# A hybrid layer on one core: first row of the batch densely through the first mixture, order and filler matmuls changed, last half row densely through the second mixture

## The reference

```
x = x + scan(norm(x))          # state space model, 16 states per feature
x = x + mixture(norm(x))       # 8 experts, top 1, capacity 512
x = x + conv(norm(x))          # two gates and one long convolution
x = x + mixture(norm(x))       # the same weights again
```

```
probs = softmax(x @ Wr + br)
gate, idx = max(probs), argmax(probs)
pos = position of the token among those of its expert, counted from 1
kept where pos < C
h = relu(gate * x @ W1[idx] + b1[idx])
out = gate * (h @ W2[idx] + b2[idx])       # 0 for tokens that aren't kept
```

## Time and profile before

| | us |
|---|---|
| median of three runs | 488.82 |
| fastest and slowest | 488.31, 494.63 |
| the profiled execution | 495.49 |
| its span, first to last instruction | 493.7 |
| busy: PE, DVE, ACT, POOL | 292.3, 343.4, 212.3, 309.2 |

### The profile page before, as it was taken

One profiled execution on the slowest core, in us unless ns is written; L12 is line 12 of the kernel. 1 busy time (PEld: TensorE's weight loads), 2 busy tenths in 40 slices (PEclk: granted clock), 3 DMA queues, 4 the chain that ended last, 5 costly groups with the idle time before them and its releaser, 6 DMA issues.

```text
span 493.7 us, 4946 instructions
## 1 busy us (share of the span) xinstructions
PE 292.3 (59%) x1327; PEld 152.8 (31%) x1327; DVE 343.4 (70%) x794; ACT 212.3 (43%) x346; POOL 309.2 (63%) x218
## 2 busy tenths in 40 slices
PE   4978753588877887970010782439778584036730
PEld 3323310312412412530000551216355583024410
DVE  4798699999999999977260763453787974236520
ACT  2787755246556646511010491334785121015610
POOL 2142189699999999957575002767745647527674
PEclk9999975587787777685555798566799896559965
DMA  7014240840100100106412342110201122132200
GB/s 212 18 69 129 60 127 0 285 195 0 43 0 0 44 0 1 44 1 174 110 44 77 110 152 74 54 43 27 68 13 33 56 66 93 38 110 80 78 23 11
DMA packets 29159, 34.12 MB, mean 69 GB/s; under 512 B 5488, under 2 KB 20862, under 8 KB 29132
## 3 DMA queue, kind: packets, MB, share of 16 engines
q1 hardware_dynamic: 24236, 25.39, 16.7%
q0 software_dynamic: 4096, 7.71, 4.9%
q10 hardware_dynamic: 800, 0.71, 0.5%
HBM read 14.43 MB, written 20.19 MB: 70 GB/s over the span
## 4 chain that ended last, share of the span: by engine, by line
DVE 26%; issue 26%; PE 20%; POOL 8%; ACT 6%; another core or an unknown queue 5%; DMA 3%; DVEq 3%; SPq 2%; ACTq 1%; POOLq 0%
DVE states L825 13%; POOL x L1157 3%; POOL states L810 2%; PE ps L1521 2%; PE ps L1592 2%; ACT scaled L1257 2%; PE ps L1611 2%; PE ps L1062 2%; DVE stats L882 1%; PE ps L691 1%; POOL slots L1036 1%; PE ps L1195 1%; SPq L1409 1%; PE ps L1211 1%
## 5 line engine op out<-in xcount | busy, mean ns | idle before, releaser
L810 POOL TENSOR_TENSOR states<-states,c_rows 128x1024 f32<-128x1024 f32 x60 | 144.5, 2440 | 18.2 <-DVE states L825 17.8
L825 DVE TENSOR_TENSOR_SCAN states<-ps,inp 128x1024 f32<-128x1024 f32 x64 | 140.5, 2261 | 0.4 <-ACT ps L786 0.4
L786 ACT ACTIVATE ps<-ps,bias_p,scale_p 128x1024 f32<-128x1024 f32 x64 | 75.0, 1177 | 64.5 <-PE ps L676 64.2
L1036 POOL DMA_INDIRECT slots<-x,put x64 | 63.9, 999 | 47.1 <-DVE put L1030 28.8
L676 PE MATMUL ps<-stack,sel 96*128 96x512 bf16 x128 | 49.6, 482 | 35.3 <-DVE states L825 35.1
L1157 POOL DMA_INDIRECT x<-answers,put x32 | 30.9, 965 | 45.5 <-DMA answers<-reply 36.5
L1348 POOL DMA_INDIRECT out<-reply,home x32 | 31.6, 988 | 24.9 <-DVE reply L1327 17.0
L691 PE MATMUL ps<-states,red 128*32 128x512 f32 x256 | 41.6, 764 | 2.5 <-POOL states L810 2.5
L1327 DVE SCALAR_TENSOR_TENSOR reply<-ps,rows,kept 128x128 f32<-128x128 f32 x64 | 18.6, 344 | 29.7 <-remote 18.0
L676 PEld LDWEIGHTS ps<-stack,sel 96*128 96x128 bf16 x128 | 8.8, 104 | 75.7 <-DVE states L825 64.7
L882 DVE BATCH_NORM_STATS2 stats<-x 128x6 f32<-128x128 f32 x96 | 19.8, 277 | 14.1 <-DMA x<-answers,put 13.9
(11 more groups left out here) (174 smaller groups left out, 604.5 us busy)
## 6 DMA issues: line engine op xcount, KB each, us to landing
slots<-zero SPq DMA_DIRECT2D x8, 528.0 KB
rows<-slots SPq DMA_DIRECT2D x16, 264.0 KB
steps<-part SPq DMA_DIRECT2D x4, 768.0 KB, 3.3
stack<-steps SPq DMA_DIRECT2D x12, 256.0 KB, 4.2
answers<-x SPq DMA_DIRECT2D x4, 512.0 KB
answers<-reply SPq DMA_DIRECT2D x8, 256.0 KB, 2.6
out<-x SPq DMA_DIRECT2D x4, 512.0 KB
x<-in_x SPq DMA_DIRECT2D x3, 512.0 KB, 5.6
```

The source lines that it names most:

```text
L786: act.activation(bank(ps, slot(b, u), 2), bank(ps, slot(b, u), 2), ACT.Exp, scale=m["scale_p"][:, group(u):group(u) + 1], bias=m["bias_p"] ...
L810: eng.tensor_tensor(h[:, u * SEQ:(u + 1) * SEQ], h[:, u * SEQ:(u + 1) * SEQ], c_rows[:, b * SEQ:(b + 1) * SEQ], ALU.mult).then_inc(done, 1)
L825: dve.tensor_tensor_scan(h[:, u * SEQ:(u + 1) * SEQ], bank(ps, slot(b, u), 2), inp[:, b * SEQ:(b + 1) * SEQ], 0.0, ALU.mult, ALU.add).then ...
L1036: pool.indirect_dma_start(out=m["slots"][n // BATCH], out_offset=bass.IndirectOffsetOnAxis(m["put"][:, b, i:i + 1], 0), in_=m["x"][:, b * ...
```

## The change

- First mixture, row 0 of the batch: it isn't scattered. All 1024 tokens go through all 8 experts as a dense product (class `Dense`): ScalarE scales the rows, TensorE turns them, and in 16 steps (2 halves of 512 tokens, 8 experts) multiplies by w1, adds -2^100 where the token isn't the expert's (a bf16 matmul with `pick`), ScalarE takes the relu, TensorE multiplies by w2 and adds up over experts in PSUM. b2 comes in by the one-hot rows in `turn_back`, and VectorE adds gate times sum to x (`finish`). Rows 1 to 3 are scattered and gathered as before.
- Second mixture: the same for the last 4 tiles (second half of row 3, 8 steps), laid between the experts; they are stored by one more DMA (`store_last`). Row 3 has 4 scatters left.
- "Natural order": each row is counted from the one-hots of all former rows (`count`); `own` and `prior` are gone.
- The first scan unit is moved ahead into `project` on TensorE, ScalarE and VectorE (`begin`).
- `keep_clock`: bf16 matmuls of ones, 128x128 by 512 columns, whose product nothing reads, at several places of TensorE's queue, 68 in all.
- The weights are loaded by SP before x of the first layer is stored, while the scan runs.
- Statistics no longer make `spread` and `neg_mean`: the moments are kept per use, eps comes in as ScalarE's bias.
- Convolution: v times filt_bias is added by TensorE (`bias_diag`, two fp32 matmuls of 512 columns per row) and the first z operation goes. The first row's products move from GpSimd to VectorE. The order of rows on TensorE, ScalarE and VectorE is changed.

The diff, cut to its core:

```diff
+def keep_clock(pe, m, ps, at, n):
+
+    ones = m["ones"][:, :].rearrange("p (o e) -> p o e", o=1).broadcast_to([P, HT, P])
+    for _ in range(n):
+        pe.matmul(bank(ps, at), m["ones"][:, :], ones, start=True, stop=True)
...
     def count(self, pe, n):
...
+        need(pe, self.placed, n)
+        for row in range(b):
+            for i in range(BT):
+                pe.matmul(counts, m["ones"][:, :], m["onehot"][:, row, i:i + 1, :].broadcast_to([P, BT, EXPERTS]), start=row + i == 0, stop=False)
         need(pe, self.hot, n + 1)
...
+    def first(self, pe, s):
+        h, e = divmod(s, EXPERTS)
+        half, at = slice(h * HALF, (h + 1) * HALF), bank(self.ps, self.HIDDEN[s % len(self.HIDDEN)])
...
+        need(pe, self.passed, self.s0 + s + 1 - len(self.HIDDEN))
+        pe.matmul(at, self.m["w1"][:, e, :], self.rows_t[:, half], start=True, stop=False)
...
+        pe.matmul(at, self.pick[:, e, :], self.not_t[:, half], start=False, stop=True).then_inc(self.pre_psum, 1)
...
+        pe.matmul(bank(self.ps, self.SUM[h]), self.m["w2"][:, e, :], self.hidden[:, s % 2, :], start=e == 0, stop=e == EXPERTS - 1).then_inc(self.added, 1)
+
+    def steps(self, pe, begin, end):
+
+        for s in range(begin, end):
+            if s + 1 < self.STEPS:
+                self.first(pe, s + 1)
+            self.second(pe, s)
...
-        dve.scalar_tensor_tensor(out=self.z[:, q, :], in0=self.v[:, q, :], scalar=self.filt_bias[:, 0:1],
-                                 in1=bank(self.ps, self.Y, 2), op0=ALU.mult, op1=ALU.add).then_inc(self.y_read, 1)
-        dve.drain()
-        dve.tensor_tensor(self.z[:, q, :], self.z[:, q, :], self.s[:, q, 0, :], ALU.mult).then_inc(self.z_done, 1)
+        dve.tensor_tensor(self.z[:, q, :], bank(self.ps, self.Y, 2), self.s[:, q, 0, :], ALU.mult).then_inc(self.z_done, 1)
...
     @plan.on("sync")
     def _(sp):
+        load_weights(sp, m, t)
+        conv.load(sp)
         for b in range(BATCH):
             need(sp, m["x_added"], 2 * b + 2)
             store_rows(sp, m, 0, b)
-        load_weights(sp, m, t)
-        conv.load(sp)
-        conv.filter_sync(sp)
-        experts.sync(sp, 0)
+        experts.sync(sp, 0, conv.filter_sync)
...
     @plan.on("tensor")
     def _(pe):
         router.count(pe, 0)
+        m["tail"]["sum"]()
+        dense.turn_marks(pe, 0)
+        dense.turn_rows(pe, 0)
+        pe.wait_ge(m["weights_in"], 16 * 5)
+        dense.first(pe, 0)
+        dense.first(pe, 1)
+        router.count(pe, 1)
+        dense.second(pe, 0)
         m["tail"]["logits"]()
+        dense.steps(pe, 1, 2)
         m["tail"]["back"]()
...
+        router.count(pe, 2)
+        dense.steps(pe, 2, 3)
+        dense.turn_rows(pe, 1)
+        dense.turn_marks(pe, 1)
+        dense.steps(pe, 3, 4)
+        router.count(pe, 3)
+        dense.steps(pe, 4, 6)
...
+        dense.turn_back(pe, 1)
+        need(pe, router.placed, BATCH)
+        need(pe, conv.mlp, 5)
+        pe.wait_ge(dense.done, 1 + CREDIT)
+        experts.tensor(pe, 0, dense.done)
...
+        late.steps(pe, 0, 2)
+
+        experts.tensor(pe, 1, between=lambda e: late.steps(pe, e, e + 1))
+        late.turn_back(pe, 0)
```

More of the change, by code:

```diff
@@ L759, in last_back @@
             back_to_tokens(BATCH - 1, 0)
-        tail["logits"], tail["back"] = last_logits, last_back
+        tail["sum"], tail["logits"], tail["back"] = lambda: sums(BATCH - 1, GROUPS + LAST_SUM + 1), last_logits, last_back
     @plan.on("scalar")
@@ L1336, in vector @@
             keep(e)
+            if between is not None and e == 0:
+                between(dve)
             if 1 <= e < self.EARLY - 1:
@@ L1708, in _ @@
+        to_router(3)
+        router.logits(pe, second(3))
         router.count(pe, second(3))
-        experts.tensor(pe, 1)
+        late.turn_rows(pe, 0)
+        late.turn_marks(pe, 0)
+        late.first(pe, 0)
+        late.steps(pe, 0, 2)
+        experts.tensor(pe, 1, between=lambda e: late.steps(pe, e, e + 1))
+        late.turn_back(pe, 0)
     @plan.on("scalar")
     def _(act):
+        dense.picks(act)
         router.row_deviations(act, 0)
+        router.probabilities(act, 0)
         m["tail"]["take_sums"]()
-        router.probabilities(act, 0)
+        dense.normalize(act, 0)
@@ L1811, in _ @@
         conv.gate_y(dve, 1)
-        routed(0)
-        added(1)
+        router.place(dve, second(0))
+        conv.add(dve, 1)
+        router.statistics(dve, second(1))
         conv.taps(dve, 3)
```

593 lines of the change are left out of this document (407 added, 186 removed).

## The result

The changed kernel took 499.22 us (median of 4 runs, 496.04 to 500.36), the kernel before, timed beside it, 491.73 (488.31 to 499.59). The ratio is 1.0135, with a 95% interval of 1.0083 to 1.0187: a little slower, within 2%. The forecast of 450 and the range of 437 to 467 were wrong, and so was a chance of 0.95 for faster.

What follows compares the result with a forecast made beforehand. VectorE bounds the scan; afterwards chains of small operations, gathers, VectorE and TensorE in turn, and GpSimd's sends. Terms of 3.8, 1.3, 10.1, 8, 7.2, 5.1 and 3 sum to 38.5: 495.5 to 457, less 6.7 gives 450; range 437 to 467.

Steps and rivals of the forecast that it cites:

- the 8 gathers less: First mixture's gathers: row 1 waits for 8 gathers instead of 16, 10.1 us off.
- the convolution's 7.2: Convolution, rows 1 to 3: fewer operations and shorter waits, less added bias_diag matmuls, 7.2 us off.
- These loads now lie in the scan: Routing, 234 to 248 us: moving weight loads removes VectorE's waits; last first-layer scatter ends at 257.6, rows ready at 263.
- Rival B: Routing, 234 to 248 us: waits aren't due to the loads, some 9 us return, 459 us; chance 0.12.
- 221 + 48 = 269: First mixture on TensorE: dense row starts at 221, takes 48 us, then expert 0 starts at 269, 3.8 us earlier.
- The sends' gain of 3: Second mixture: with TensorE busy, GpSimd idles less for replies between sends, 3 us off.
- The 8 of the hidden row 0: Convolution: row 0's work runs under the answers' stores and gathers, so row 1's streams gain 8 us.
- The start: Start of the scan: first scan unit runs in VectorE's idle time, gain 2.2 us, counted within the 3.8 to expert 0.
- A: Rival: unnamed waits come back elsewhere in strict queues, so the convolution's 7.2 and sends' 3 aren't gained, 460 us; chance 0.27.
- C: Rival: all goes well in dense row, convolution and sends, 434 us, with half of it, 442, given; chance 0.20.
- D: Rival: convolution's row 0 isn't hidden behind the experts and meets row 1 as before, 463 us; chance 0.08.
- E: Rival: TensorE's clock stays at its lower level in the dense steps, slower at 514 us; chance 0.03.

Runs made afterwards that it cites:

- a_same: The changed kernel run again without any edit: 459.20 us, ratio 0.955 to the kernel before.
- b_same: The kernel before run again without any edit, beside the unchanged changed kernel: 484.26 us.
- b_loads: The kernel before with only the loads of the experts' and convolution's weights moved into the scan: 482.97 us, ratio 0.999.
- a_quiet: The changed kernel with GpSimd's indirect scatters, gathers and sends replaced by plain DMAs to and from consecutive rows: 456.91 us, with before at 496.78.
- a_extra: The changed kernel with 24 more indirect scatters, which nothing reads, behind the last one of layer 1: 520.75 us.
- a_again: The changed kernel, unchanged, run a third time: 498.47 us, with before at 493.06, ratio 1.011.
- a_traffic: The changed kernel with 16 unread DRAM-to-DRAM copies of 2 MB added on ScalarE's queue after the scan: 536.40 us.
- b_traffic: The kernel before with 16 unread DRAM-to-DRAM copies of 2 MB added on ScalarE's queue after the scan: 569.87 us.
- a_nofill: The changed kernel without its 68 unread filler matmuls (keep_clock emptied): 471.35 us, ratio 0.976 to before at 483.77.

## Why the prediction was wrong

The stages, as differences between the milestones of the earlier trace rows, the fences above and the same instructions in the timelines, changed minus before, in us. "Late" sets the first two profiles against each other, "quiet" a_same against b_same:

```
stage                                  predicted    late   quiet
to expert 0 on TensorE                    -3.8     +16.0    -0.7
expert 0 to first gather                  -1.3      -1.5    -0.8
first gather to row 1's statistics       -10.1      -9.5    -9.4
these to row 1's streams                  -8        -5.7    -5.0
streams to last row placed                -7.2      +1.8    -8.2
placed to last scatter                    -5.1      -5.1    -7.0
last scatter to first send                 0        +4.0    +3.8
first to last send                        -3        -1.3    -0.7
last send to end                           0        +4.2     0.0
sum                                      -38.5      +2.8   -28.0
```

Late is the difference of the spans, 493.7 and 496.5; quiet that of 485.5 and 457.5, where the medians, 482.95 and 459.20, differ by 23.8. The quiet column flatters the change: the profiled execution of b_same took 487.31, 3 above its median, and began its first scan 4.85 later than the earlier trace rows. Its first row therefore hides two things. Up to the first scan the changed kernel gained 10.0, and from there to expert 0 it lost 9.4 (217.6 us against 208.2). The same piece lost 21.4 on the late one (233.9 against 212.6), where 1.4 was predicted (269 - 55 against 212.6).

Of the 41.3 us between the sums -38.5 and +2.8, 19.8 lie ahead of expert 0, 9.0 between row 1's streams and the last row's placing, 4.0 between the last scatter and the first send, and 4.2 behind the last send.

**Where the count of operations held.** The length of a dense step (2.2 against 2.23), the first tile stage, the 8 gathers less (9.4 to 9.5 of 10.1) and the 4 scatters less (5.1 and 7.0 of 5.1) came out on both kinds of occasion, and the first scatter began 2 us late (229.00 and 229.17, 227 predicted). On the quiet one the convolution's 7.2 came too (8.2), and expert 0 was 3.7 later than the 269 forecast.

**The step that failed: "In 234 to 248 VectorE [...] waits for nothing that the profile shows [...] while SP loads the weights. These loads now lie in the scan."** I took the waits of this stretch as caused by the loads and thus removed. b_loads shows that moving the loads changes nothing on a quiet occasion, b_same that the stretch is gone without moving them, and the changed kernel's 240 to 255 that it is there on a late one with the loads moved. Rival B had that right, and the view that speaks for it was at hand: the other unnamed waits of before (5.18 us in front of the last logits) have no loads beside them but GpSimd's scatters. I had not looked for what all of them share.

**With it fell the term "221 + 48 = 269" for the dense row.** The steps were right in themselves, but the chain runs under 24 scatters, in which signals come late. On the quiet occasion it ends at 272.65, on the late one at 288.83. Before the change TensorE stood idle there (0.52 of 14.00 us busy) and a late signal met slack. After it, TensorE's chain is the one that sets expert 0. The differences point the same way from the streams to the last placing (-8.2 quiet, +1.8 late) and for the end, where VectorE waits 7.42 us for a late step's result and has it at 492.50, when the last send (489.64) is over. Reckoned from the first scan on, late minus quiet, before pays 13 us (433.5 to 420.4) and the changed kernel 39 (441.6 to 402.4). That its stretches under indirect DMAs pay is shown by a_quiet and a_extra, one execution each; the split of the 26 us among them is read from the table, and no run tests it stage by stage.

**Mis-sized on both.** "Last scatter to first send: nothing changes" cost 3.8: the late steps stand in TensorE's queue ahead of expert 0, whose rows were scaled from 405.94 on and turned only at 410.95. The sends' gain of 3 was 0.7 to 1.3: on the quiet occasion they already stood 1.33 us apart in before (41.20 for 31 in b_same), so there was little idle time to win; on the late one the changed kernel's stood 1.46 apart (45.12). The 8 of the hidden row 0 were 5.0, since on a quiet occasion this piece took before only 11.90, not the 16.97 of the earlier trace rows. So where before had these waits in its trace, I had counted some of them as the change's gain. Two sums of the prediction are off without consequence: 227 + 30.2 is 257.2, not 257.6, and the "other 7.9" of GpSimd's idle time (17.0 - 9.12) still holds the 3.66 named beside it, so 4.2 are left.

**The start.** The first scan came at 54.90, as worked out (55), but gained 0.4, not 2.2, at the second scan (63.14 against 63.55). Against b_same, whose second scan is at 68.40, it gained 5.1: the start of before isn't the same in every execution, and the earlier trace rows shows the faster one. The softplus behind it took 3.42 us instead of the 1.23 of the earlier trace rows, beside GpSimd's first multiply (57.27, 2.35 us), which the earlier scan had released. This is the rule of the Trainium skill, "SBUF — State Buffer", section "SBUF: two separate sides", which I had used for the z operation and not here. For z it held as well: with one operand in PSUM all four took 1.21 to 1.23 us, in before up to 3.085.

**The rivals.** A and B named the right things (unnamed waits come back; the stretch isn't the loads), at 460 and 459. Both priced only what before had shown of such waits, and neither what a longer chain on TensorE would pay. C, D and E didn't come: row 0 was hidden, and the clock was 0.94 from 255 to 289. On a quiet occasion 459 lies in the range, some 9 off the forecast, but that is partly luck: before was at 483 there, not 489, and the gain was 23.8, not 38.5.

## What to carry to other kernels

Waits that nothing in the profile releases can be a finding and not only a gap in the record: see first what they have in common in time, and run the unchanged kernel again, on another occasion, before a change is credited with removing them. A stage in which an engine stands idle can hide late signals; whoever fills it with a chain on another engine pays for them (here expert 0 came 16 us later than before on a late occasion and 0.7 earlier on a quiet one), and work under indirect DMAs should have slack. Every experiment needs the kernel it is compared with on the same occasion: three runs in a row looked like gains of 28 to 38 us, and against the changed kernel at 459.20 none was a gain and two were losses of 7 and 12. A single profile of a kernel can also differ from the next by 5 us at its start.

## What the runs showed of the hardware

- On some occasions (before at 491 to 497 us) the engines get signals and instructions late while GpSimd's indirect DMAs are in flight: results of TensorE are read 7.0 to 8.4 us after their end (342.03 behind 334.99 in a_again, 277.04 behind 268.61 in a_extra), and instructions of TensorE come one by one on steps of about 0.7 us (242.59, 244.00, 244.72, 246.83, 247.58 and 250.36 in the changed kernel's first profile). On others the same text shows none of it, and one chip number showed both. What makes an occasion late stays open; I didn't find it in the trace. So does whether the signals or the instructions behind them are late.
- Plain DMAs by GpSimd with as many packets on the same queue don't do this (1.5 us of such waits in a_quiet, one execution), nor do 32 MB of copies on ScalarE's queue add to it as far as a_traffic and b_traffic show. The Trainium skill, "Runtime: NRT & Kernel Launch", section "Instruction fetch mechanics", says that fetching code is mostly hidden. On quiet occasions the trace agrees (1.5 us of unreleased waits); on late ones it doesn't settle it, since from 235 to 255 in the changed kernel's first profile no packet of an instruction queue was under way.
- Without the fillers the first scan begins at 60.00, with them at 55.06. From 40 to 55 us TensorE's granted clock is 0.85 in the one and 1.00 in the other: for 12.2 us in all, unread products paid here. At the start they guard against a drop that not every execution has: without fillers the clock of this stretch was 1.00 in before's first profile (first scan at 60.23) and 0.85 in b_same's (65.08).

```profile
40.00:55.00 15.00, 13.87 (x42) 6.15 (x42) 11.71 (x16) 11.95 (x19) 2.15 (x1) 1.00 0.37 107
```

```profile
40.00:55.00 15.00, 10.52 (x25) 4.37 (x23) 11.06 (x13) 10.40 (x15) 2.12 (x1) 0.85 0.35 105
```

The first is a_same, the second a_nofill; the columns are those of the earlier trace rows.
